# Constant multiplications on TensorE between the ring items ahead of attention

## The reference

```
block 1: hawk recurrence (gate * scan(x_in, a)) @ w_out.T, then silu(h2 @ w_mlp_gate.T) * (h2 @ w_mlp_up.T) @ w_mlp_down.T
block 2: FFN with 8 LoRA experts, top 2 of softmax(h @ gate_w.T + gate_b)
block 3: attention, 16 heads of 8 channels:
         attn = softmax(q @ k.T * 128**-0.5) + rel_bias[i - j]
         out  = layernorm(attn @ v) * ln_gamma + ln_beta
block 4: the FFN of block 2 once more
```

## Time and profile before

| | before |
|---|---|
| timed runs, median of 3 | 734.91 us |
| profiled execution, its own time | 739.95 us |
| its span | 738.1 us |
| mean granted TensorE clock over the span | 0.963 of full |
| PE busy | 678.5 us (92%) |
| DVE busy | 534.6 us (72%) |
| ACT busy | 381.4 us (52%) |
| POOL busy | 104.7 us (14%) |

### The profile page before, as it was taken

How to read it: one execution, slowest core, us unless ns; L and a number is a source line. 1 busy time by engine, 2 the same in 40 slices (tenths; PEclk the granted TensorE clock), 3 DMA queues, 4 the chain that set the end, 5 groups by cost and what they waited for, 6 DMA issues and landing times.

```text
span 738.1 us, 10734 instructions
## 1 busy us (share of the span) xinstructions
PE 678.5 (92%) x3302; PEld 267.5 (36%) x3302; DVE 534.6 (72%) x956; ACT 381.4 (52%) x687; POOL 104.7 (14%) x100
## 2 busy tenths in 40 slices
PE   6998999999787799999999899999999998988997
PEld 4453545444343122232332222332322322324543
DVE  5579787648699858868868758868788688308744
ACT  3734223325012146757767557766667677882231
POOL 5920211001037110020020020020100202002000
PEclk9999999999779679999999899999999999999999
DMA  8000000001213112012011030030020000000000
GB/s 254 4 0 0 2 0 1 1 0 39 93 65 104 58 39 85 2 49 75 6 56 63 22 103 3 18 100 8 32 91 3 1 1 2 2 1 0 1 28 28
DMA packets 21414, 26.61 MB, mean 36 GB/s; under 512 B 3312, under 2 KB 12016, under 8 KB 21360
## 3 DMA queue, kind: packets, MB, share of 16 engines
q1 hardware_dynamic: 20496, 25.39, 10.7%
q0 software_dynamic: 144, 0.52, 0.2%
q10 hardware_dynamic: 720, 0.00, 0.1%
HBM read 21.52 MB, written 4.19 MB: 35 GB/s over the span
## 4 chain that ended last, share of the span: by engine, by line
PE 70%; DVE 19%; ACT 4%; issue 2%; DMA 2%; DVEq 1%; POOL 1%; SPq 1%; POOLq 0%; ACTq 0%
PE banks L1432 18%; PE banks L1355 16%; PE banks L1418 14%; DVE negmax L1032 6%; PE banks L1158 6%; PE banks L1236 4%; PE banks L1279 3%; PE banks L1369 2%; PE banks L1227 2%; PE banks L1171 2%; DVE arena L890 1%; ACT arena L735 1%; DVE arena L940 1%; DVE stats L787 1%; PE banks L1382 1%
## 5 line engine op out<-in xcount | busy, mean ns | idle before, releaser
L1032 DVE TENSOR_REDUCE negmax<-banks 128x1 f32<-128x1024 f32 x256 | 301.2, 1218 | 71.0 <-PE banks L1355 69.6
L735 ACT ACTIVATE arena<-banks 128x512 f32<-128x512 f32 x512 | 271.9, 601 | 149.1 <-PE banks L1418 145.6
L1355 PE MATMUL banks<-arena 72*128 72x512 bf16 x512 | 162.6, 403 | 23.2 <-DVE negmax L1032 20.0
L1418 PE MATMUL banks<-arena 75*128 75x512 bf16 x512 | 161.7, 387 | 6.6 <-ACT arena L735 3.1
L1432 PE MATMUL banks<-arena 128*32 128x512 f32 x1024 | 139.6, 618 | 0.7 <-ACT arena L735 0.7
L1355 PEld LDWEIGHTS banks<-arena 72*128 72x128 bf16 x512 | 38.1, 100 | 164.5 <-DVE negmax L1032 75.0
L1418 PEld LDWEIGHTS banks<-arena 75*128 75x128 bf16 x512 | 48.8, 99 | 96.4 <-ACT arena L735 48.3
L1236 PE MATMUL banks<-arena,bT 128*128 128x512 f32 x128 | 60.1, 593 | 1.6 <-ACT arena L589 1.6
L499 POOL TENSOR_TENSOR rstd<-veps,neghalf 128x4 f32<-128x4 f32 (+1 forms) x24 | 27.1, 1129 | 241.7 <-DVE veps L806 189.9
L589 ACT ACTIVATE arena<-banks 128x512 f32<-128x512 f32 (+1 forms) x56 | 32.1, 595 | 50.4 <-PE banks L1158 21.5
L890 DVE TENSOR_SCALAR arena<-banks,bi 128x512 f32<-128x512 f32 x32 | 23.8, 745 | 33.0 <-PE banks L1236 33.0
(11 more groups left out here) (130 smaller groups left out, 635.6 us busy)
## 6 DMA issues: line engine op xcount, KB each, us to landing
arena<-qk_scratch SPq DMA_DIRECT2D x192, 48.0 KB
arena<-in_tab SPq DMA_DIRECT2D x8, 1024.0 KB, 6.7
qk_scratch<-arena SPq DMA_DIRECT2D x8, 384.0 KB, 2.8
out<-x SPq DMA_DIRECT2D x4, 256.0 KB, 2.3
x<-in_x SPq DMA_DIRECT2D x1, 512.0 KB, 4.6
x<-in_x POOLq DMA_DIRECT2D x1, 512.0 KB, 7.7
arena<-nm_part SPq DMA_DIRECT2D x24, 8.0 KB, 1.9
w_aT<-in_w_aT SPq DMA_DIRECT2D x1, 256.0 KB, 6.6
```

The source lines that it names most:

```text
L735: act.activation(probs[s % 2][:, h, :], score_bank(g, n), ACT.Exp, scale=SCALE).then_inc(exp_done, 1)
L1032: return dve.tensor_reduce(negmax[:, buf, k:k + 1], slot.rearrange("p a b -> p (a b)"), axis=AXX, op=ALU.max, negate=True)
L1355: last = pe.matmul(slot[:, half_, :], qs[0:STACK, buf, h, t * P:(t + 1) * P], ks[0:STACK, buf, h, half_ * HALF:(half_ + 1) * HALF], start= ...
L1418: pe.matmul(score_bank(g, n), ks[0:DEPTH, g % BUFS, h, t * P:(t + 1) * P], qs[0:DEPTH, g % BUFS, h, q * HALF:(q + 1) * HALF], start=True, ...
```

## The change

A multiplication of `ident` by `ones` into the first 128 columns of bank 7 is issued 14 times ahead of item 0, twice after each of items 0 to 11 and 27 to 36, 8 times after V.0.0 and 12 times ahead of the first step of attention. So that bank 7 is free for it, dense results from O0.1.1 on take turns on banks 4 to 6, and TensorE waits once until the last result in bank 7 (`HB0.1.1.3`) is emptied.

```diff
@@ -75,6 +75,7 @@
 BUSY_SCAN, BUSY_ROUTE = 13, 8
+BUSY_LOADS, BUSY_STATS, BUSY_ITEM, BUSY_START = 14, 8, 2, 12
@@ -148,7 +149,7 @@
         if name == FIRST_BESIDE_RING:
-            turn, turns = 0, [4, 5, 6, 7]
+            turn, turns = 0, [4, 5, 6]
@@ -175,6 +176,7 @@
+LAST_IN_SPARE = [n for n, _ in JOBS[:INDEX[FIRST_BESIDE_RING]] if BANK[n] == 7][-1]
@@ -1468,16 +1470,27 @@
+            def keep_busy_spare(n):
+                for _ in range(n):
+                    pe.matmul(pv_bank[:, 0:P], ident[:], ones[:], start=True, stop=True)
+
             def fill_up_to(done, stop):
                 for k in range(done, stop):
                     fill_ahead(k)
+                    if k < TURN_BEFORE or k >= CS_BEFORE:
+                        keep_busy_spare(BUSY_ITEM)
                 return stop
+
+            pe.wait_ge(*emptied(LAST_IN_SPARE))
+            keep_busy_spare(BUSY_LOADS)
 
             done = fill_up_to(done, R_BEFORE)
             back("O0", "R0", 1, 1)
             for h in range(2):
                 done = fill_up_to(done, V0_BEFORE[h])
                 value_half(0, h)
+                if h == 0:
+                    keep_busy_spare(BUSY_STATS)
@@ -1493,6 +1506,7 @@
             pe.wait_ge(*emptied("CS.1"))
+            keep_busy_spare(BUSY_START)
             for s in range(FIRST):
```

## The result

The change makes the kernel faster: median 733.76 us of 22 runs against 736.76 of 22 for the kernel before, a ratio of 0.9946 with an interval of 0.9928 to 0.9965. That is 4.0 us (2.6 to 5.3), where 5.9 were forecast. The sign and the mechanism held; the size was too large by half. The range was stated for a kernel before at 734.91 us, the median of its first three runs; on that base the ratio gives 730.9 us, inside 724.5 to 733.5. The plain median of 733.76 us lies just above it, since the kernel before also has a higher median (736.76) over its 22 runs.

A forecast was written before the change was run, and what follows sets the result against it. At full clock VectorE sets the pace of attention's preparation; at half clock TensorE has almost no room left. Terms of -1.6 and -5.4 sum to -7.0 us; with 1 us taken off, 734.9 - 5.9 = 729.0 us, range 724.5 to 733.5.

The forecast's parts named there:

- (a): Ahead of item 0: the 14 multiplications fit into 3.20 us of idle time, and item 0 gains 0.45 us.
- (b): Items 0 to 11 and the eight after V.0.0: fillers hide under VectorE's reductions; gain about 1.15 us.
- (c): Items 12 to 26, without fillers: the clock fall at 236.4 and VectorE's 1.63 us wait come again; zero.
- rival 2: Larger gain: the fall at 236.4 (1.5 us) or at 420 (3.2 us) goes too; 724.3 to 727.5, chance 0.14.
- (d): Items 27 to 36 with two fillers: the clock stays full, VectorE sets the time; zero by itself.
- (e): The twelve before the first scores are on the path: first score at 253.65, not 252.20; 1.45 us lost.
- (f): First attention steps at full clock: step 3 begins at 262.1 instead of 267.49; 5.4 us gained, (e) included.
- The 1 us taken off for the timed runs: Deduction from the forecast gain, because the timed runs may lack some of the profile's time at half clock.
- rival 3: No change: in timed runs attention's start reached full clock by about 256 by itself; -2.0 us, 732.9, chance 0.12.
- Bank 7 and the waits: Dense results without bank 7 in their rotation, and the new wait on HB0.1.1.3: zero cost each.
- Rival 4: Slower: the clock falls around 247 anyway and stays at half through the fillers; +4.9 us, 739.8, chance 0.06.
- A clock of 0.50 anywhere after the twelve: Sign that the prediction is wrong: half clock at any point behind the fillers before the first scores.

The follow-up runs named there:

- banks only: The change with all its multiplications taken out, leaving the rotation over three banks and the wait for bank 7; 0.9999 of the kernel before.
- back only: The changed kernel with only the pairs behind items 27 to 36 and the twelve kept; 0.9964 of the kernel before.
- the turn's ten: The changed kernel with ten more multiplications at the end of the attention loop's body; 0.9997 of the kernel before.
- both versions written out with fewer fillers: The changed kernel with its attention loop as plain code on all engines, without the twelve (729.7 us) or with 12, 8, 2, 6 (725.5 us).
- two more looped profiles: The change without its multiplications (0.9999), and the kernel before with ten multiplications at the loop's turn (1.0054).
- third profile: The same changed kernel, profiled and timed a third time; 0.9944 of the kernel before.
- first repeat: The same changed kernel, profiled and timed a second time; 0.9935 of the kernel before.

## Why the prediction was right, and where it was off

*(a) The fourteen hide and item 0 comes 0.45 us sooner.* Not shown: against the profile before it came 0.31 us sooner (196.66 to 196.35), but the profiles of banks only and back only, without the fourteen, have 196.18 and 196.30. The load is not fixed at 195.54: it released item 0 at 195.17, 195.60 and 196.86 in profiles without the fourteen. With them it can come late as well (197.53 without the twelve, 0.42 us behind the fillers). In the changed kernel's first profile item 0 followed the fillers at once at 195.64, so its data had arrived, 0.5 us earlier if they came as in banks only. What a full clock saves on the item, the overrun of the fillers can take back. Back only had no need of it: its clock fell only at 196.16, when item 0 was through.

*(b) 1.15 us from items 0 to 11.* Right, a little more: from the first reduction to the rest of QK.1.0.0 it took 23.59 us before and 22.09 after, 1.50.

*(c) The fall at 236.4 comes again.* Wrong in the first profile and in four others that have the fillers of items 0 to 11 and 27 to 36, right in three (half clock from about 237.8 to 241.2 with the turn's ten and in both versions written out with fewer fillers; 55.53 - 53.95 = 1.6 us and 54.36 - 52.53 = 1.8 us in two of them). Where it stays away another 1.5 us is gained: CS.1 is taken 40.69 us behind the first reduction and not 43.70. It was my rival 2, priced at 1.5.

*(d) Items 27 to 36 are VectorE's, zero.* Right: from the sum for CS.1 to the end of the split of the maxima it takes 8.51 us, before (240.36 to 248.87) and after (237.04 to 245.55), and VectorE waits for nothing.

*(e) The twelve cost 1.45 us.* Right: 1.43, by leaving them out.

*(f) Steps at full clock, 8.45 us from first score to step 3 in place of 15.3.* The mechanism is right, the size off: 250.31 to 260.10 is 9.79. I had VectorE set the pace without a pause, but TensorE does at the end: VectorE waits 0.40 us twice for an item that TensorE fills behind a weighing, the second time for the item of 259.44, behind the weighing of 258.44, which the first score of step 3 follows. 5.5 us gained, not 6.85.

Together, 1.50 + 1.51 - 1.43 + 5.50 = 7.08 us, which is 79.64 - 72.56. The errors of (a), (c) and (f) cancel in the profile, so that it comes so near to the forecast of 7.0 is luck.

*The 1 us taken off for the timed runs* is the term that failed most; it was a guess, and too small. The profile before had 55 us at half clock, the median execution 47, and two more looped profiles of that work took 76.78 and 77.96 us where this one took 79.64. Against their mean of 78.1 the change saves 5.6 us. Of rival 3, that the timed runs lack part of the stretch at half, this is the weaker form: it shortens the gain and doesn't end it.

From 5.6 to 4.0 the marks name two candidates. The profiles of the kernel before and of banks only have a mean span of 735.9 us, the three of the changed kernel 731.8: 4.1 us, which is what the timed runs say. It comes from 5.7 us saved between first reduction and fifth weighing, 0.5 lost ahead of it and 1.2 lost up to the last weighing, at the turn.

The loss ahead of the first reduction shows in the other profiles too. "Ahead" is 196.2 to 198.0 us in the five without the front's fillers. Four of them had the clock at half from 65 to 69; that fall is free, as the changed kernel's third profile had it too and came to 196.38. With front fillers six of nine profiles had a fall from 74 on instead, and came 1.4 to 1.9 us late (74 to 78) or 2.7 to 3.3 (to 81): the nine have a mean of 197.9, the five of 196.8. Three of these six, and no other profile with all of the change's pairs, also had the fall at 237. Executions with both falls are the likely ones among the 17 at a clock of 0.984 to 0.986, but no trace of one of them exists. Why an addition at 192 should go with a fall at 74 isn't shown; with nine profiles against five it may be chance. The same holds for the longer fall at the turn, in three profiles against two.

*Bank 7 and the waits:* nothing that the runs of banks only can tell. *Rival 4* (slower) didn't occur: no profile with the twelve had a clock below full between them and the turn. "A clock of 0.50 anywhere after the twelve" was too wide a sign of being wrong: it came, at the turn, where the kernel before has it too.

## What to carry to other kernels

Multiplications of constants can hold TensorE's clock where the work is paced by another engine, though not in every execution, and cost nothing as long as they end before the wait that they fill; count them for the earliest arrival, not for the one that the profile shows. Price a clock fall by what it delays: 34 us less at half clock bought 4 us here, since VectorE set the pace in much of that time. And where the clock is the subject, one profile is one draw: read several, or the clocks of the timed runs, before taking a fall's length as the kernel's own.

## What the runs showed of the hardware

With the same instructions, the clock stayed at half through 20 us of unbroken attention work (254 to 274, 0.51) in one profile, 14 us in the kernel before, some 9 us with banks only (first score at 250.81, half clock until 260.18) and 7 us without the twelve (251 to 259, 0.57). The Trainium skill ("TensorE: Matmul & The Clock Gate", Part 1) says that sustained activity releases the throttle; by these rows work without a pause isn't enough by itself, and what kind of work it takes wasn't tried apart. It also says that the number of slow matmuls at a kernel's start varies from run to run; the traces agree (the first 28 records of TensorE, from 3.47, took 5.29 us in the profile before and 6.11 in the changed kernel's first repeat), and show the same in the middle of a kernel.

The loop's turn costs TensorE 2.2 to 3.0 us of idle time here (412.33 above). Ten multiplications put ahead of it cover none of that without the change (2.21 us left) and at most 1.0 to 1.4 us with it (1.68 left of 2.64 to 3.04); written out, it is gone.
